# Turning keys and queries with crosswise ScalarE copies, and spreading scales in two fp32r rounds

## The reference

```python
H, KVH, D, CHUNK = 32, 8, 128, 128
def apply_rope(x, cos, sin):
    rot = concatenate([-x[..., 64:], x[..., :64]], axis=-1)
    return x * cos + rot * sin
q, k = apply_rope(x @ Wq.T), apply_rope(x @ Wk.T)       # 4 query heads share one key head
v = x @ Wv.T
# per chunk of 128 tokens: scores, decay, state carried from chunk to chunk
y = (q k^T * decay) (v dt) + (q exp(G)) state
y = y / sqrt(mean(y^2) + eps) * gnorm_w * silu(x @ Wg.T)
out = y @ Wo.T
```

## Time and profile before

| | |
|---|---|
| median of 3 runs | 2130.53 us (2129.3 to 2133.38) |
| the profiled execution: time, span | 2131.05 us, 2129.2 us |
| TensorE busy | 2009.1 us (94%) |
| VectorE busy | 1630.6 us (77%) |
| ScalarE busy | 1117.0 us (52%) |
| GpSimd busy | 879.7 us (41%) |
| mean granted clock of TensorE | 0.98 |
| chain that ended last, by engine | PE 84%, DVE 8%, ACT 3% |

### The profile page before, as it was taken

How to read it: one execution, slowest core, us unless ns; L and a number is a source line. 1 busy time by engine, 2 the same in 40 slices (tenths; PEclk the granted TensorE clock), 3 DMA queues, 4 the chain that set the end, 5 groups by cost and what they waited for, 6 DMA issues and landing times.

```text
span 2129.2 us, 31978 instructions
## 1 busy us (share of the span) xinstructions
PE 2009.1 (94%) x9216; PEld 1508.5 (71%) x9216; DVE 1630.6 (77%) x2905; ACT 1117.0 (52%) x2347; POOL 879.7 (41%) x705
## 2 busy tenths in 40 slices
PE   5799999999999999999899999999999999988992
PEld 3577777777777777767677777777777777777881
DVE  5887777777777777757877777777777777747996
ACT  5455555555555555452455555554555455537881
POOL 2243433434343434343254444343434444434661
PEclk9999999999999999999999999999999999999996
DMA  6322121212121212135121212121212121228778
GB/s 252 101 58 54 47 60 49 59 44 64 38 68 37 69 39 69 39 88 180 50 70 40 70 39 66 38 69 35 69 39 69 39 69 38 61 85 274 230 230 325
DMA packets 147515, 182.05 MB, mean 86 GB/s; under 512 B 12935, under 2 KB 89319, under 8 KB 147454
## 3 DMA queue, kind: packets, MB, share of 16 engines
q1 hardware_dynamic: 137310, 155.52, 25.2%
q0 software_dynamic: 8704, 25.21, 3.3%
q10 hardware_dynamic: 1440, 0.58, 0.1%
HBM read 152.90 MB, written 28.37 MB: 85 GB/s over the span
## 4 chain that ended last, share of the span: by engine, by line
PE 84%; DVE 8%; ACT 3%; DMA 2%; issue 2%; POOL 1%; SPq 0%; DVEq 0%; ACTq 0%; POOLq 0%
PE PJ L1223 14%; PE PJ L1225 14%; PE PJ L1224 13%; PE SC L1356 5%; PE OU L1223 5%; PE OU L1224 5%; PE OU L1225 5%; PE CS L1366 4%; PE YE L1377 3%; PE YI L1223 2%; DVE gm L1776 2%; PE OU L1319 2%; PE YI L1224 2%; PE YI L1225 2%; PE TR L1306 1%
## 5 line engine op out<-in xcount | busy, mean ns | idle before, releaser
L470 POOL TENSOR_TENSOR zl<-yb,zh 128x512 fp32r<-128x512 f32 x122 | 157.8, 1294 | 351.5 <-ACT zh L972 350.6
L756 POOL TENSOR_TENSOR gm<-gbc,amask 128x512 f32<-128x512 f32 x128 | 180.3, 1408 | 170.6 <-DVE wfl L1837 155.0
L1223 PE MATMUL OU<-woh,zh 128*128 128x512 f32 x488 | 226.6, 464 | 1.2 <-POOL zl L470 1.2
L1223 PE MATMUL PJ<-xnh,wqh 128*128 128x512 f32 x544 | 221.8, 408 | 4.5 <-DVE t L1765 2.7
L1223 PE MATMUL PJ<-xnh,wgh 128*128 128x512 f32 x512 | 221.1, 432 | 3.6 <-POOL wgl L726 3.6
L1225 PE MATMUL PJ<-xnh,wql 128*128 128x512 f32 x544 | 213.6, 393 | 0.0
L1224 PE MATMUL PJ<-xnl,wqh 128*128 128x512 f32 x544 | 213.5, 392 | 0.0
L972 ACT ACTIVATE zh<-yb 128x512 fp32r<-128x512 f32 x122 | 76.6, 628 | 250.3 <-PE OU L1225 181.3
L1225 PE MATMUL PJ<-xnh,wgl 128*128 128x512 f32 x512 | 203.4, 397 | 0.0
L1224 PE MATMUL PJ<-xnl,wgh 128*128 128x512 f32 x512 | 202.9, 396 | 0.0
L1868 DVE TENSOR_TENSOR yb<-YI,yb 128x512 f32<-128x512 f32 x96 | 66.4, 691 | 175.6 <-PE YI L1225 175.4
(11 more groups left out here) (551 smaller groups left out, 5338.6 us busy)
## 6 DMA issues: line engine op xcount, KB each, us to landing
gbc<-decay_exponents SPq DMA_DIRECT2D x128, 256.0 KB, 4.8
stage<-in_wq SPq DMA_DIRECT2D x72, 256.0 KB, 3.7
stage<-in_wg SPq DMA_DIRECT2D x64, 256.0 KB, 2.6
stage<-in_wo SPq DMA_DIRECT2D x64, 256.0 KB, 2.6
gbc<-in_wm SPq DMA_DIRECT2D x48, 256.0 KB
stage<-in_wkv SPq DMA_DIRECT2D x34, 256.0 KB, 2.6
experts<-in_wm SPq DMA_DIRECT2D x16, 512.0 KB, 5.6
experts<-expert_rows SPq DMA_DIRECT2D x16, 512.0 KB, 14.2
```

The costliest lines, as they stand in the source:

```text
L470: nc.gpsimd.tensor_tensor(lo[:], yb[:, c, :], hi[:].bitcast(F32), ALU.subtract).then_inc(S["zlo"], 1)
L756: g.tensor_tensor(gm[:, c % 2, :].rearrange("p (h i) -> p h i", h=HG), gbc[:, c % 2, :].rearrange("p (h i) -> p h i", h=HG), amask[:].unsq ...
L1223: nc.tensor.matmul(out_, a_hi, b_hi, start=first, stop=False)
```

## The change

Four things change.

- ScalarE's new `cross(i)` copies the two halves of the raw projection crosswise from PSUM into `turned` (two instructions). VectorE's `rope` then takes three passes (cosine from PSUM; sine in place, in SBUF; add) and not four (cosine, two sine halves from PSUM, add), and waits for the copies ahead of the first. `roperd` is signalled by the sine pass as before.
- The scales become a high part (ScalarE copies `zhf` rounded into `rmsh`) and a low part (VectorE subtracts, `scales_low`), and the spread takes two rounds of four fp32r products in place of four fp32 products.
- On ScalarE `weighted(0)` and `key_rows` stand ahead of `z_hi(0)`.
- TensorE's spread waits for the low part, `z_hi(0)` too.

```diff
+        rmsh, rmsl = ql[:, 0, :], ql[:, 1, :]
...
                 a.activation(zhf[:], zhf[:], ACT.Exp, scale=-0.5).then_inc(S["rms"], 1)
+                at.before("spread", 1)
+                at.wait("rms", 1)
+                a.activation(rmsh, zhf[:], ACT.Copy).then_inc(S["rmshi"], 1)
...
+                        def cross(i):
+                            turned = qf[:, i - 1, :] if i else kf
+                            bank = PJ[(0, 0, 1, 0, 1)[i]]
+                            at.wait("proj", (1, 3, 4, 5, 6)[i])
...
+                            hd = D // 2
+                            a.activation(turned[0:hd, :], bank[hd:D, :], ACT.Copy)
+                            a.activation(turned[hd:D, :], bank[0:hd, :], ACT.Copy).then_inc(S["cross"], 1)
...
                                 weight_hi(0)
                                 weight_hi(1)
+                                cross(0)
                                 if not first:
                                     rms_batch(at, half)
+                            cross(1)
                             v_hi()
                             weight_hi(2)
+                            at.wait("coef", 1)
+                            weighted(0)
+                            cross(2)
+                            key_rows()
                             if not first:
                                 z_hi(at, 0)
                             weight_hi(3)
-                            at.wait("coef", 1)
-                            weighted(0)
-                            key_rows()
+                            cross(3)
                             decay(0)
+                            cross(4)
                             if not first:
                                 z_hi(at, 1)
...
             def spread_scales(at):
-                at.wait("rms", 1)
+                at.wait("rmslo", 1)
...
-                for c in range(NCH):
-                    cs = slice(c * SUMS, (c + 1) * SUMS)
-                    ins = nc.tensor.matmul(TOU[c][:], pick[cs, :], zhf[cs, :], start=True, stop=True)
+                for part in (rmsh, rmsl):
+                    for c in range(NCH):
+                        cs = slice(c * SUMS, (c + 1) * SUMS)
+                        ins = nc.tensor.matmul(TOU[c][:], pick[cs, :].bitcast(F32R), part[cs, :], start=part is rmsh,
+                                               stop=part is rmsl)
...
+            def scales_low(at):
+                at.wait("rmshi", 1)
+                v.tensor_tensor(rmsl, zhf[:], plain(rmsh), ALU.subtract).then_inc(S["rmslo"], 1)
...
-                            hd = D // 2
+                            at.wait("cross", i + 1)
                             v.tensor_tensor(t1[:], PJ[bank][:], cosb[:], ALU.mult)
-                            v.tensor_tensor(turned[0:hd, :], PJ[bank][hd:D, :], sinb[0:hd, :], ALU.mult)
-                            v.tensor_tensor(turned[hd:D, :], PJ[bank][0:hd, :], sinb[hd:D, :],
-                                            ALU.mult).then_inc(S["roperd"], 1)
+                            v.tensor_tensor(turned, turned, sinb[:], ALU.mult).then_inc(S["roperd"], 1)
                             at.wait("roperd", i + 1)
                             v.tensor_tensor(turned, t1[:], turned, ALU.add).then_inc(S["rope"], 1)
...
+                            if not first:
+                                scales_low(at)
                             rope(1, 0)
                             if not first:
                                 late_z(at, 0)
                                 late_z(at, 1)
                             rope(2, 1)
```

More of the change, by code:

```diff
@@ L307, in build @@
             proj=10, tr=2, score=4, cstate=3, yinter=3, yintra=4, ssq=1, spread=1, oproj=4,
-            vraw=1, vhi=1, kn=1, dec=4, expg=3, vw=3, whi=4, tanh=4, ysq=4,
-            rsln=1, rms=1, zhi=4,
+            vraw=1, cross=5, vhi=1, kn=1, dec=4, expg=3, vw=3, whi=4, tanh=4, ysq=4,
+            rsln=1, rms=1, rmshi=1, zhi=4,
             coef=1, roperd=5, rope=5, wsc=4, wlo=4, stt=3, yt=3, y=4, gated=4, u=4, z=4, accd=4,
-            vlo=1, gmask=4, zlo=4,
+            vlo=1, gmask=4, zlo=4, rmslo=1,
         )
-        LAGGED = {"ssq", "spread", "oproj", "rsln", "rms", "zhi", "z", "accd", "zlo"}
+        LAGGED = {"ssq", "spread", "oproj", "rsln", "rms", "rmshi", "rmslo", "zhi", "z", "accd", "zlo"}
         S = {k: sem("s_" + k) for k in per_step}
@@ L1024, in square @@
                             a.activation(rs[:, c, :], yb[:, c, :], ACT.Square).then_inc(S["ysq"], 1)
+                        def cross(i):
+                            turned = qf[:, i - 1, :] if i else kf
+                            bank = PJ[(0, 0, 1, 0, 1)[i]]
+                            at.wait("proj", (1, 3, 4, 5, 6)[i])
+                            if i == 0:
+                                at.before("score", 4)
+                                at.before("tr", 2)
+                            elif i == 1:
+                                at.before("yinter", 3)
+                            hd = D // 2
+                            a.activation(turned[0:hd, :], bank[hd:D, :], ACT.Copy)
+                            a.activation(turned[hd:D, :], bank[0:hd, :], ACT.Copy).then_inc(S["cross"], 1)
                         def v_hi():
@@ L1753, in rope @@
                             at.wait("proj", (1, 3, 4, 5, 6)[i])
[L1754 to L1757, removed]
                             if i:
```

## The result

The kernel after the change takes 2141.14 us (median of 7 runs, 2139.54 to 2146.93), the kernel before in the same comparison 2130.53 (7 runs). The ratio is 1.0055, with a 95% interval of 1.0042 to 1.0069: slower by about 10.6 us. The forecast was 2149, its range 2128 to 2157. The sign and the range held; the sum behind them did not, as the stages show.

A forecast was written before the change was run, and what follows sets the result against it. It took a step to last TensorE's own work plus what holds TensorE up. 30 steps x 0.57 us plus 1 us for the flushes gave 18.1, on 2131.05: 2149 us, range 2128 to 2157.

The forecast's parts named there:

- The race for the second sine pass: In each loop step GpSimd's zl0 takes the shared port 0.2 us before VectorE's second sine pass, delaying q3; chance 0.42.
- The rival for the race lost: Sine pass beats zl0; later collisions delay the last add and scores(0), +0.4 a step, 2144 us; chance 0.27.
- The first steps: First step of each half: same collisions meet an earlier q3 and a shorter VectorE queue, about 0.
- 0.57 a step: In each of 30 loop steps scores(0) starts at 683.66, 0.57 us later than before.
- The spread's gain: TensorE's spread takes 0.56 us instead of 1.07, so TensorE is 0.5 us earlier from there to scores(0).
- The walk: The turns of one loop step followed instruction by instruction, with row durations and port waits, up to scores(0) at 683.66.
- Arrive within 0.1: VectorE's last add and TensorE reach scores(0) within 0.1 us; anything making either later costs 30 times.
- The flushes: In each half's flush the copy and subtraction add 1.44 us, the spread falls from 2.03 to 1.1: +0.5 each.
- if neither q3 nor scores(0) waits: Sign against the forecast: with no wait at q3 or scores(0) in the loop, the time falls by about 15 us.

The follow-up runs named there:

- e4: Kernel before with the new two-round fp32r spread alone, turns as before: 2121.35 us, ratio 0.9960.
- e5: Kernel after with the old fp32 spread, keeping the new turns: 2141.88 us, ratio 1.0041.
- e2: Kernel after, in half 2's first step cross(0), cross(1), v_hi ahead of the weight copies, later weight copies behind cross(2), cross(3): 2136.84 us, ratio 1.0032.
- e10: Kernel after with GpSimd's second decay mask early, and old four-pass turns, order and no crosswise copies in each half's first step: 2117.93 us, ratio 0.9939.
- e9: Kernel after with z_hi(0) ahead of key_rows on ScalarE, so zl0 reaches GpSimd before the second sine pass: 2149.34 us, ratio 1.0088.
- e3: Kernel after with GpSimd's second decay mask moved directly behind the first, ahead of the queries' turns: 2122.94 us, ratio 0.9966.
- e7: Kernel before with only GpSimd's second decay mask moved directly behind the first: 2131.46 us, ratio 0.9999.
- e6: Kernel after with GpSimd's second decay mask early and, in half 2's first step, crosswise copies ahead of the late weight copies: 2118.22 us, ratio 0.9931.

## Why the prediction was right in sign and range, and wrong in its sum

The sign and the range came true by luck. The race that the forecast is built on went the other way; the rival's course of things happened, at 0.06 a step instead of 0.4, and the 26 steps together bring 1.6 us, less than the 4.3 that the prediction itself calls no change. What made the kernel slower lies in a place that the prediction put at nothing.

**The first steps: the step that failed.** The prediction put them at "about 0", from a q3 that is earlier and a VectorE queue that is shorter. It looked at the engine that waits and not at the queue of the engine that is now waited for. The diff shows cross(0) behind weight_hi(0) and weight_hi(1); in the first step of half 2 these wait for loads, and VectorE's new wait for `cross` passes that on to the key's turn, to TensorE's next projection and to all behind it. Measured: +9.7 in that step (4.4 to 9.7 over the traces), -1.8 in the next (which e4 and e5, with one part of the change each, have too: 54.50 and 53.91 for 55.90; why, no run shows). Moving the copies alone brings the step to 58.49 in e2, and in e10, where no copies are made there, it is 58.36, against 55.64 to 57.65 with the old turns.

**0.57 a step: mis-sized, it measured 0.06.** Three pieces:

*The spread's gain* was put at 0.5; it is 0.40 (0.67 us instead of the estimate of 0.56). That the row groups overlap in fp32r was right, and that the Copy and the subtraction fit ahead of the spread was too: the subtraction ends at 668.85 + 0.69 = 669.54, the spread starts at 669.83.

*The race for the second sine pass* was given to zl0 by 0.2 us, with 0.42 for that and 0.27 for the other way. It went the other way by 0.25. The walk had the half copies 0.49 apart, the spacing of full copies; at 0.60 the two pairs ahead of z_hi(0) make zl0 later, 673.75 on the clock of before and not 673.5. And it had each sine pass 0.70 behind its cosine pass, where it follows at 0.61 (670.81 to 671.42); so the second sine pass, walked to 673.69, came at 673.50. The first cosine pass, walked to 668.66, came at 668.66. Where zl0 is first, e9, q3 waits 0.96 instead of the 1.15 forecast and the step grows by 0.42 instead of 0.57. A lead of 0.2 at the end of a walk with terms taken from other shapes was no ground for a point forecast of 18 us.

*The rival for the race lost* is what happened. It had the right place, scores(0), and the right collisions up to the last turn (the second add lasts 1.67, the third sine pass 1.77), and the wrong price, +0.4. It let zl1 hold the last sine pass, so that the add would end at 683.5. In the trace the sine pass is first, holds zl1 for 0.36 and the add then waits for zl1: it ends at 685.27, 683.12 on the clock of before. scores(0) is 0.09 later than before, and not 0.46.

**"Arrive within 0.1" was a misreading** of the earlier trace rows. Two engines that arrive together need not be independent: the add's end hung on zl1, zl1 on out_proj(0). e4 shows it, with the full 0.40.

**Shown right:** collisions of VectorE and GpSimd as the reason for the lost gain. By the Trainium skill's "SBUF — State Buffer", section "SBUF: two separate sides", a VectorE instruction with two SBUF inputs and a GpSimd instruction that reads SBUF share a pair of ports, and the one that starts first keeps the other out for its whole length. The traces agree for the new sine pass (it waits 1.16 behind zl's start in e9) and for GpSimd (zl waits 0.36 for a sine pass already under way); but the block ends 1.15 us into the 1.30 of GpSimd's instruction, not at its end. With one GpSimd instruction moved out of the queries' turns the kernel after gains 0.61 a step (e3), the kernel before nothing (e7). Of the 0.55 that e3 is below before, 0.40 is the spread's and 0.15 the new turns'. The flushes came out at +0.6, priced at +0.5. And if neither q3 nor scores(0) waits, the prediction said, the time falls by about 15: e3's loop is such a case, 26 steps of 0.55 and so 14.3, and e6, which mends part of the first step too, is at 0.9931 of before.

## What to carry to other kernels

When work moves from one engine to another, read the receiving queue at every place where the program is written out, the first and last steps above all: what stands ahead of the moved instruction there, and what that waits for, is now on the path. When two engines seem to arrive together, ask what ended the later one; if it hangs on the other, the two move together. And before a pass is moved from PSUM to SBUF inputs, look which GpSimd instructions lie beside it: here one of them, left in its old place, cost 0.61 a step, and the new turns gain 0.15 without it.

## What was not expected of the hardware

ScalarE's copies of 64 partitions from one half to the other follow each other at 0.60 us, full copies of 128 partitions from PSUM at 0.49, with durations of 0.59 and 0.60. Here half the data took no less time. fp32r products in four row groups of 32 overlap as fp32 ones do: a round takes 0.34 us (669.83 to 670.17). And a scores(0) that TensorE had to wait for, even by the 0.08 of before, takes 0.10 longer to the next product, 0.96 (683.09 to 684.05) instead of the 0.86 of e3.
